# Queries stored by tile and dimension in DRAM, between the projection and the attention of one kernel

## The reference, cut to what matters

```python
xn = layernorm(x, g_in)                                    # (8, 512, 512)
q = (xn @ Wq).reshape(b, n, H, DH).transpose(0, 2, 1, 3) * scale   # 16 heads of 64
sim = jnp.einsum('bhid,bjd->bhij', q, k) + bias            # 513 columns: a null key comes first
attn = jax.nn.softmax(where(masked, neg, sim), axis=-1)
out = jnp.einsum('bhij,bjd->bhid', attn, v)
```

## Time and profile before

| | us |
|---|---|
| median of 3 runs | 1877.23 (1870.98 to 1877.26) |
| the profiled execution, its own time | 1879.36 |
| its span, first to last instruction | 1877.3 |
| PE busy in the span | 1684.0 (90%) |
| ACT waiting for a store of queries (L440) | 116.0 in 40 waits |
| DMA packets | 220248, 301.83 MB |
| stores `q_hi_d`, `q_lo_d` | 64 each, 256.0 KB, 2.6 and 2.9 from issue to landing |
| loads of `queries`, `queries_and_ones` | 32 each, 512.0 KB, 5.3, 7.4 and 9.3 from issue to landing |

### The profile page before, as it was taken

The page is one execution under the profiler, slowest core; times in us unless marked ns, Lnnn a source line. Parts: engine busy times, 40 slices in busy tenths (PEclk is TensorE's granted clock), DMA queues, the critical chain, the costliest instruction groups (busy, mean ns, idle before and its releaser), DMA issues. The chain is left out here.

```text
span 1877.3 us, 37692 instructions
## 1 busy us (share of the span) xinstructions
PE 1684.0 (90%) x10388; PEld 1374.0 (73%) x10389; DVE 1040.0 (55%) x3148; ACT 721.6 (38%) x1884; POOL 782.8 (42%) x1459
## 2 busy tenths in 40 slices
PE   6899967999999999997988894499999998999998
PEld 5677756887877877876777773387777886888886
DVE  5444445786776776775455555643333343455555
ACT  2222215676676666765122221033333343221221
POOL 1000326676686676774455555422222221223323
PEclk9999987998999998998999996599999999999999
DMA  6566659697787877783333333334565332223423
GB/s 228 177 228 219 218 170 250 166 228 164 166 214 179 182 201 159 200 199 94 115 134 132 129 130 150 158 99 169 184 226 210 106 106 91 87 93 123 145 90 112
DMA packets 220248, 301.83 MB, mean 161 GB/s; under 512 B 15201, under 2 KB 128401, under 8 KB 218082
## 3 DMA queue, kind: packets, MB, share of 16 engines
q1 hardware_dynamic: 189986, 235.20, 43.5%
q0 software_dynamic: 11280, 35.99, 6.4%
q10 hardware_dynamic: 18864, 29.38, 4.5%
HBM read 187.26 MB, written 113.26 MB: 160 GB/s over the span
## 5 line engine op out<-in xcount | busy, mean ns | idle before, releaser
L789 ACT ACTIVATE probs<-scores,lowest 128x514 f32<-128x514 f32 (+3 forms) x512 | 281.9, 555 | 25.5 <-DVE lowest L716 24.8
L688 POOL TENSOR_SCALAR probs<-probs,rsums 128x512 f32<-128x512 f32 (+3 forms) x512 | 264.9, 523 | 0.0
L716 DVE CUSTOM_DVE_ANT_0 scores<-psum,resident 128x514 f32<-128x514 f32 (+3 forms) x512 | 245.8, 489 | 25.7 <-issue 19.9
L842 PE MATMUL psum<-ident,probs 128*128 128x128 f32 x1280 | 249.9, 294 | 9.1 <-POOL probs L688 8.9
L831 PE MATMUL psum<-keys,queries 128*128 (+4 forms) x640 | 230.8, 369 | 27.5 <-DMA queries_and_ones<-q_hi_d 19.6
L858 PE MATMUL psum<-probsT,v_now 128*64 128x128 f32 x2560 | 205.2, 290 | 9.8 <-DVE probsT L730 7.2
L842 PEld LDWEIGHTS psum<-ident,probs 128*128 128x128 f32 x1280 | 149.7, 143 | 63.4 <-issue 35.4
L831 PE MATMUL psum<-keys_lo_and_mask,queries_and_ones 128*128 (+4 forms) x640 | 192.6, 310 | 0.0
L797 ACT ACTIVATE probsT<-psum 128x128 f32<-128x128 f32 (+3 forms) x256 | 111.9, 437 | 186.5 <-PE psum L842 184.1
L858 PEld LDWEIGHTS psum<-probsT,v_now 128*64 128x64 f32 x2560 | 139.2, 140 | 52.8 <-issue 34.8
L730 DVE COPY probsT<-psum 128x128 f32<-128x128 f32 (+3 forms) x256 | 125.3, 489 | 84.6 <-PE psum L842 79.9
(11 more groups left out here) (221 smaller groups left out, 3813.8 us busy)
## 6 DMA issues: line engine op xcount, KB each, us to landing
ys_d<-y_out ACTq DMA_DIRECT2D x72, 256.0 KB, 2.0
q_hi_d<-q_hi SPq DMA_DIRECT2D x64, 256.0 KB, 2.6
q_lo_d<-q_lo SPq DMA_DIRECT2D x64, 256.0 KB, 2.9
queries<-q_hi_d SPq DMA_DIRECT2D x32, 512.0 KB, 5.3
queries<-q_lo_d SPq DMA_DIRECT2D x32, 512.0 KB, 7.4
queries_and_ones<-q_hi_d SPq DMA_DIRECT2D x32, 512.0 KB, 9.3
oT_d<-o_out SPq DMA_DIRECT2D x64, 256.0 KB, 5.3
o_in<-oT_d SPq DMA_DIRECT2D x32, 512.0 KB, 3.8
```

The costliest lines, as they stand in the source:

```text
L688: pool.tensor_scalar(out=row, in0=row, scalar1=rsums[:, n % RING:n % RING + 1], scalar2=1.0, op0=ALU.mult, op1=ALU.mult).then_inc(probs_sc ...
L716: dve.tensor_tensor_reduce(out=scores[n % 4][:, 0:CK[i]], in0=score_psum(i, n), in1=bias_of(resident, i, h), scale=1.0, scalar=3.0e38, op0 ...
L789: act.activation(probs[n % RING][:, 0:CK[i]], scores[n % 4][:, 0:CK[i]], ACT.Exp, bias=lowest[:, n % 4:n % 4 + 1], scale=-1.0, accum_out=s ...
L842: last = pe.transpose(probsT_bank[n % 2][:, j * P:(j + 1) * P], probs[n % RING][:, AHEAD + j * P:AHEAD + (j + 1) * P], ident[:])
```

## The change

The two DRAM tensors become (B, TB, DH, H * P): for each tile of 128 tokens and each dimension, one row of 8 KB with 16 heads x 128 tokens. A load of queries then reads 64 rows of 8 KB. A store of a tile n of the projection holds two heads, and they land in different columns, so each half of 64 partitions is its own DMA: 64 x 4 pieces of 512 bytes. The semaphore counts are doubled accordingly.

```diff
-        "q_hi": nc.dram_tensor("q_hi_d", (B, INNER, S), F32, kind="Internal").ap(),
-        "q_lo": nc.dram_tensor("q_lo_d", (B, INNER, S), F32, kind="Internal").ap(),
+        "q_hi": nc.dram_tensor("q_hi_d", (B, TB, DH, H * P), F32, kind="Internal").ap(),
+        "q_lo": nc.dram_tensor("q_lo_d", (B, TB, DH, H * P), F32, kind="Internal").ap(),
@@ store_q, stage_project
                     for name, half in (("q_hi", q_hi), ("q_lo", q_lo)):
-                        sp.dma_start(dram[name][bass.ds(b, 1), n * P:(n + 1) * P, :].rearrange("a p s -> p (a s)"),
-                                     half[:, n % 2, :].bitcast(F32)).then_inc(q_stored[n % 2], 16)
+                        for h in range(2):
+                            sp.dma_start(dram[name][bass.ds(b, 1), :, :, (2 * n + h) * P:(2 * n + h + 1) * P].rearrange(
+                                             "a i d p -> d (a i) p"),
+                                         half[h * DH:(h + 1) * DH, n % 2, :].rearrange("d (i p) -> d i p", i=TB).bitcast(F32)
+                                         ).then_inc(q_stored[n % 2], 16)
@@ end of the stage, SP
-                sp.wait_ge(q_stored[k], 16 * IC * B)
+                sp.wait_ge(q_stored[k], 32 * IC * B)
@@ copy_q, ACT
-                    act.wait_ge(q_stored[n % 2], 32 * (IC // 2 * b + n // 2))
+                    act.wait_ge(q_stored[n % 2], 64 * (IC // 2 * b + n // 2))
@@ load_queries, stage_attend
-                    sp.dma_start(dst.bitcast(F32), dram[name][bass.ds(b, 1), :, i * P:(i + 1) * P].rearrange(
-                        "a (h d) p -> d (a h) p", d=DH)).then_inc(queries_loaded[i % 2], 16)
+                    sp.dma_start(dst.rearrange("d h p -> d (h p)").bitcast(F32),
+                                 dram[name][bass.ds(b, 1), i].rearrange("a d n -> d (a n)")
+                                 ).then_inc(queries_loaded[i % 2], 16)
```

## The result

The kernel takes 1901.94 us after the change (median of 4 runs, 1897.97 to 1906.27) against 1875.35 us (4 runs) of the kernel before on the same chip: a ratio of 1.0140, with an interval of 1.0116 to 1.0165, or +26.6 us. The forecast was 1920, +42 us. Direction and place were right; the size was 1.6 times too large, and the cause was another one.

What follows compares the result with a forecast made beforehand. PE was taken as the bound, with the stores of queries already on its path. Stores +34 us, clock +9 and loads -1 made +42 on 1879.4, 1921; given as 1920 for a median, range 1888 to 1950.

Steps and rivals of the forecast that it cites:

- So the stores are on the path already: Projection: late stores of queries hold ACT's copies, then kv_out and k_hi, then PE's transposition of V; PE waits 13.8 us.
- The price of a 512-byte piece, +1.55 us per tile: Projection's stores: a tile takes 2.85 us of DMA time instead of 1.30, 99 us over the stage.
- The issues ... I cost it at nothing: Projection, SP: four issues per tile, some 1.5 us, keep up; the last starts 0.8 us later, under 2.85 us of transfer.
- Half rate at half height: Projection's stores: 64 partitions reach only 8 of 16 ports, so halved stores run at about half rate; 8 KB loads stay.
- Batches 1 to 5, +4.8 each: Projection: six longer stores ahead of copy 7 add 9.3 us, 4.5 absorbed by idle DMA time; +24 for five batches.
- Batch 6, +2: Projection: no load of x, and 2.85 us of stores nearly hidden by PE's 2.8; only the biases push, +2 us.
- Batch 7, +4: Projection: runs after a delay; copies 2 to 7 took 10.3 us, five steps at 2.85 take 14.3, +4 us.
- The clock, +9: Starts of projection batches: longer PE waits drop the granted clock to 0.50; 3 x 2.7 us plus 1.2, +9 us.
- The loads, -1: Attention: loads of queries are hidden except the first tile's three transfers, which get faster in 8 KB rows, -1 us.
- not slower: Rival, projection's stores: 512-byte pieces cost no more than 2 KB rows, first loads run at full rate; 1874 us, chance 0.12.
- The stores fit into the idle time: Rival, projection: 12 us of DMA idle per batch absorbs two thirds of the added time; +14, 1893 us, chance 0.2.
- Scattered writes: Rival, projection: scattered stores are slower than scattered loads, twice 2.85 us per tile; near 2040 us, chance 0.08.

Runs made afterwards that it cites:

- four places: q_hi and q_lo get four buffer places instead of two: on the changed kernel 1862.05 us (0.9923), on the kernel before 1858.71 us (0.9892).
- The cut alone: Kernel before, old layout and 2 KB rows, with each store of queries issued as two DMAs of 64 partitions: 1897.55 us, 1.0122.
- the loads alone: Kernel before with only the attention's loads of queries read as 8 KB rows, stores unchanged, values mixed up: 1874.95 us, 0.9997.
- The run with half of the bytes: Kernel before with stores split into 64-partition DMAs, storing only the first 256 tokens of each row (1 KB): 1884.62 us, 1.0044.

## Why the prediction was right in place and wrong in cause

- *"So the stores are on the path already"*: right. The time came where the prediction put it, by way of ACT's wait, `k_hi` and PE's transposition. Its tests held: ACT's wait above 150 (158.2), PE's near 35 (34.7), a stretch of query stores below 200 GB/s (168), more time at clock 0.50. One sign that it had named for being wrong showed, stores at 300 GB/s or more: they went at 338 GB/s in after itself when several were queued, and the 168 are the pace of the tiles. Another, an attention over fewer us, is there with 2.0 us. Two tests failed: of batches 1 to 5 only two were longer by 4 to 7 us, and PE's first wait wasn't shorter. That the wait for the place carries the cost is shown by taking the wait away: with four places the new layout is at 0.9923 of the kernel before and the old one at 0.9892, 0.3% apart instead of 1.4%.
- *The price of a 512-byte piece, +1.55 us per tile*: this term was wrong in its cause and is the one that was mis-sized. The store's 2.85 us were taken from loads on 64 partitions. The same pieces at full height run at 344 GB/s and cost nothing (0.9998). Both rows behind the price were read past their other columns. The 170 GB/s were moved at a DMA share of 0.60, so the engines idled for part of that microsecond. And 184 GB/s on 64 partitions stand beside 199 for 2 KB rows on 64 partitions: between these two the piece makes 8%, and the rest of the way to 404 is the half height. The forecast had the right sign and about the right place by luck: the cut into halves brought a delay of the same kind, a longer cycle of the place, for another reason.
- *"The issues ... I cost it at nothing"*: this is the step that failed. It took 0.33 to 0.38 us for an issue from DMAs of 128 partitions. At 64 partitions an issue takes 0.55 us in 2 KB rows and 0.60 to 0.70 in 512-byte pieces, so four take 2.4 to 2.8 us per tile instead of 1.5. And they aren't hidden under the transfer: each store lands some 2.5 us after its own issue, so the last issue's start sets the landing, and it is 2.1 us behind the first instead of 0.4. The prediction had 0.8 us for this delay and put it under 2.85 us of transfer; it is 1.8 us, and it stands in the place's cycle in full. That the price of one issue is higher at 64 partitions it could have read before. The kernel's stores of K are of 64 partitions, and SP's timeline of the kernel before shows them at 1.6 times the price of the earlier trace rows:

```profile
57.05 0.58 SPq L233 DMA_DIRECT2D k_hi_d<-k_hi  x1
57.68 0.59 SPq L233 DMA_DIRECT2D k_lo_d<-k_lo  x1
```

The sentence *"it would show as 0.8 us per pair of tiles"* named the right place with under half of the size: the undisturbed cycle grew from 4.27 to 6.16 us. That SP keeps up was right for a whole batch: with four places it does, at 3.0 us per tile.
- *Half rate at half height* (the Trainium skill, *SBUF — State Buffer*, "Door 1: The DMA port swizzle"), which the prediction weighed as another way to the same result: the trace agrees for single transfers. The 8 KB loads into 64 partitions moved 217 GB/s, a little over the 199 of 2 KB rows and about half of 404. It doesn't cap stores that queue up: 338 GB/s with both halves in the queue, in after. Where SP feeds the halves one by one it shows in the DMA engines' share. The cut alone needed 0.80 of them for 184 GB/s, and the kernel before 0.66 for 251:

```profile
144.00:150.00 6.00, 6.00 (x27) 4.86 (x26) 4.61 (x16) 1.20 (x2) 1.21 (x2) 1.00 0.80 184
```
```profile
256.00:260.00 4.00, 4.00 (x19) 3.21 (x18) 1.12 (x3) 1.20 (x2) 0.00 (x0) 1.00 0.66 251
```

But a half-height store has half of the bytes, and it lands no later after its issue than a whole one, 2.4 us against 2.6 and 2.9 in the medians.
- *Batches 1 to 5, +4.8 each*: they came to +15.5 together, clock included, against 24 and most of 9. A smaller rate was foreseen, but stores catch up at 338 GB/s whenever a load of `x` has made them queue, which the estimate at a flat 184 left out. *Batch 6, +2*: it was +6.7. The step took PE's 2.8 us per tile to hide 2.85; a cycle of 6.2 us for two tiles has no cover there. *Batch 7, +4*: +2.1. *Batch 0, +4*: +4.5.
- *The clock, +9*: the mechanism was right; 40.8 us at 0.50 instead of 17.0 are 24 us more at half speed, at most 12 us of PE's work. They overlap with waits, so their part in the +28.8 can't be read off by itself, and no run held the clock fixed.
- *The loads, -1*: right within the measurement (0.9997). PE's first wait was 1.4 us shorter with the loads alone, and 0.7 us longer in after.

The rivals: *not slower* came close to its condition (stores at 350 GB/s, 338 to 344 seen), was right that the piece costs next to nothing, and was still wrong about the time, since its mechanism left the cut out. *The stores fit into the idle time* named 1893, 9 us under the result; the stores catch up in part, as it says. *Scattered writes* did not happen.

**What stays open.** That the time goes by way of the place's cycle is shown, and that its growth lies between the first and the last issue. How many of the cut's 22 us would go if only the half-height transfer ran at full rate isn't known: 128 KB at 199 GB/s are 0.66 us and at 404 GB/s 0.33, so by this estimate it is 0.3 us of a cycle of 5.7, which lies just above PE's 5.6. The run with half of the bytes takes that much off, but bytes off the whole stage as well, and the run that added issues without bytes disturbed the stores. No run issued half of the stores from another engine, or at full height four at a time, so the number of issues and their price weren't varied one without the other. Why a 64-partition issue takes longer than a 128-partition one isn't shown.

## What to carry to other kernels

Before changing a layout for longer rows on one side, count what it does to the other side's DMAs: how many there are, and on how many partitions each, since the number of issues and their height cost here 22 to 31 us where the length of the pieces cost none. Compare the cycle of a buffer's place (filled, stored, free) with the pace of the engine that the place must not hold: at best 4.3 or 4.7 us against 5.6 gave the same time, and 6.2 cost 1.4% of the kernel. The best case under the pace isn't enough, though, when loads lengthen some cycles. Where the profile shows a wait for a place, try more places first: here that took 1.1% off the kernel before, and the change of layout, 1.4% without it, was then 0.3%. And read a rate together with the share of time in which the DMA engines were busy: 170 GB/s at 0.60 and 168 at 0.72 were no limits.

## What the hardware showed that was not expected

- The stores of queries took SP 0.33 to 0.46 us per issue at 128 partitions and 0.55 to 0.70 at 64, and 64 partitions of 4 bytes took 0.60, so it isn't the bytes. It isn't the partitions alone either: the first load of weights, 128 partitions, took 0.50 in the kernel before. A load of 4 bytes to each of 64 partitions in after's own timeline:

```profile
304.42 0.60 SPq L655 DMA_DIRECT2D null_col<-in_cond  x1
```

- 512-byte pieces written from 128 partitions reached 344 GB/s in queued stores, 85% of the 404 of 2 KB rows; read into 64 partitions they had 184 GB/s, 92% of the 199 of 2 KB rows there.
- Stores of 64 partitions that alternate between the lower and the upper half reached 338 GB/s together when several were queued, while loads into one half had 199 to 217.
- Three DMAs of 64 times 4 bytes to DRAM per tile moved the landing of the 256 KB stores behind them from 2.6 to 8.7 us, and the kernel from 1877 to 2092 us.
